# Softmax totals of a gated cross-attention block: the cross-partition sum moved from two 512-column matmuls to VectorE and two 16-column matmuls

## What is computed

```
x = x + tanh(g_xattn) * attention(layernorm(x), ctx, ctx, mask)

q, k, v = query @ Wq, key @ Wk, value @ Wv        # 32 query heads, 8 key heads, size 128
logits  = 30 * tanh(rope(q) . rope(k) * 0.0884 / 30)
logits  = where(mask, logits, -1e30)
weights = softmax(logits, axis=-1)                # needs the sum of exp over the keys
attn    = weights @ v ; return attn @ Wo
```

## Time and profile before

| | us |
|---|---|
| median of 3 runs | 819.16 |
| lowest and highest | 818.01, 819.62 |
| the profiled execution, device time | 819.05 |
| its span in the profile | 817.3 |

### The profile page before, as it was taken

The page is one execution under the profiler, slowest core; times in us unless marked ns, Lnnn a source line. Parts: engine busy times, 40 slices in busy tenths (PEclk is TensorE's granted clock), DMA queues, the critical chain, the costliest instruction groups (busy, mean ns, idle before and its releaser), DMA issues.

```text
span 817.3 us, 12587 instructions
## 1 busy us (share of the span) xinstructions
PE 785.6 (96%) x3937; PEld 654.8 (80%) x3937; DVE 586.6 (72%) x1224; ACT 355.4 (43%) x722; POOL 492.8 (60%) x392
## 2 busy tenths in 40 slices
PE   4889999999999999999999999999998689999998
PEld 3777888888888888888888888888887468888786
DVE  7797777777777777777777777776787677787531
ACT  3665444444334444444443443434444345555420
POOL 3689765566555666655665566656887466566400
PEclk9999999999999999999999999999999899999999
DMA  8320302010210201020102101120020034442011
GB/s 286 108 78 17 115 1 78 1 52 1 78 54 1 78 1 52 1 78 0 55 1 78 52 0 43 35 47 1 1 62 0 25 88 103 101 111 49 1 65 39
DMA packets 56989, 41.61 MB, mean 51 GB/s; under 512 B 22922, under 2 KB 44298, under 8 KB 56938
## 3 DMA queue, kind: packets, MB, share of 16 engines
q1 hardware_dynamic: 56938, 40.90, 17.3%
HBM read 38.77 MB, written 2.11 MB: 50 GB/s over the span
## 4 chain that ended last, share of the span: by engine, by line
PE 91%; DVE 5%; POOL 2%; issue 1%; ACT 1%; DMA 0%; DVEq 0%; POOLq 0%
PE ps_o L53 8%; PE ps_o L55 8%; PE ps_o L54 7%; PE bank_q L55 7%; PE bank_q L53 7%; PE bank_q L54 7%; PE ps_qT L1141 3%; PE bank_kv L53 3%; PE bank_kv L54 3%; PE bank_kv L55 3%; PE ps_s L54 3%; PE ps_s L53 3%; PE ps_s L55 3%; PE ps_pv L53 2%; PE ps_pv L54 2%; PE ps_pv L55 2%
## 5 line engine op out<-in xcount | busy, mean ns | idle before, releaser
L522 POOL TENSOR_TENSOR aT_lo<-attn,aT_hi 128x512 fp32r<-128x512 f32 x64 | 96.6, 1510 | 168.4 <-ACT aT_hi L691 168.4
L651 ACT CAST qT_hi<-ps_qT 128x512 fp32r<-128x512 f32 x64 | 37.5, 585 | 169.7 <-PE bank_kv L1142 90.0
L53 PE MATMUL bank_q<-wq_hi,xT_hi 128*128 128x512 f32 x256 | 107.7, 421 | 1.0 <-DVE wq_lo L819 1.0
L53 PE MATMUL ps_o<-wo_hi,aT_hi 128*128 128x512 f32 x256 | 100.6, 393 | 2.5 <-POOL aT_lo L522 1.8
L55 PE MATMUL bank_q<-wq_hi,xT_lo 128*128 128x512 f32 x256 | 102.3, 400 | 0.0
L54 PE MATMUL bank_q<-wq_lo,xT_hi 128*128 128x512 f32 x256 | 102.3, 400 | 0.0
L55 PE MATMUL ps_o<-wo_hi,aT_lo 128*128 128x512 f32 x256 | 99.9, 390 | 0.0
L54 PE MATMUL ps_o<-wo_lo,aT_hi 128*128 128x512 f32 x256 | 99.8, 390 | 0.0
L507 POOL TENSOR_TENSOR probs<-probs,keepT 128x512 f32<-128x512 f32 x64 | 83.1, 1299 | 13.0 <-ACT probs L667 13.0
L535 POOL TENSOR_TENSOR roped<-q_cos,q_sin 128x512 f32<-128x512 f32 x61 | 78.8, 1293 | 1.8 <-DVE q_sin L840 1.7
L911 DVE TENSOR_TENSOR qT_lo<-ps_qT,qT_hi 128x512 fp32r<-128x512 f32 x64 | 44.2, 691 | 43.4 <-ACT kT_hi L652 43.4
(11 more groups left out here) (233 smaller groups left out, 2209.5 us busy)
## 6 DMA issues: line engine op xcount, KB each, us to landing
wo_raw<-in_Wo SPq DMA_DIRECT2D x8, 1024.0 KB, 5.4
wq_raw<-in_Wq SPq DMA_DIRECT2D x7, 1024.0 KB, 5.7
packed<-in_gate_q SPq DMA_DIRECT2D x40, 64.0 KB, 2.3
packed<-in_up_q SPq DMA_DIRECT2D x40, 64.0 KB, 2.3
packed<-in_down_q SPq DMA_DIRECT2D x10, 256.0 KB, 3.4
acc<-in_x SPq DMA_DIRECT2D x8, 256.0 KB, 8.1
wkv_raw<-in_Wk SPq DMA_DIRECT2D x8, 256.0 KB, 5.9
wkv_raw<-in_Wv SPq DMA_DIRECT2D x8, 256.0 KB, 6.3
```

Of the source, the lines that this page charges most:

```text
L53: nc.tensor.matmul(out, w_hi, m_hi, start=first, stop=False)
L522: nc.gpsimd.tensor_tensor(aT_lo[:], attn[:], aT_hi[:].bitcast(F32), ALU.subtract).then_inc(a_split, 1)
L651: nc.scalar.copy(qT_hi[:], ps_qT[:])
```

## The change

The sum over the keys is taken in two steps. VectorE transposes the masked `probs` in blocks of 32x32 (into `r_tot`), which brings the 32 keys of a block of partitions onto the columns, and sums each group of 32 columns: a tile `partial` of 16 columns, in which row 32g + r holds what key group g gives to query r of each block of 32 queries. It is split into `partial_hi` and `partial_lo` on VectorE. A 128x128 matrix `fold` (one where row and column agree modulo 32, built on VectorE out of the identity at the start) sums the four key groups in two matmuls of 16 columns. The totals arrive in `ps_tot` already in the layout that the block transpose L960 made before, so that transpose goes and the reciprocal reads `ps_tot` directly. The new VectorE work stands behind `p_lo` and ahead of q's rotary products in the queue; TensorE waits for it (`p_summed`) ahead of the totals, and for `fold` ahead of its first slot, in place of `ones`. New semaphores are left out below.

```
@@ tiles
-        ones = sb("ones", [P, P], F32R)
+        fold = sb("fold", [P, P], F32R)
+        partial = sb("partial", [P, GC // 32], F32)
+        partial_hi = sb("partial_hi", [P, GC // 32], F32R)
+        partial_lo = sb("partial_lo", [P, GC // 32], F32R)
@@ GpSimd, start
-                nc.gpsimd.memset(ones[:].bitcast(F32), 1.0).then_inc(ones_done, 1)
@@ ScalarE, cap_and_exp
                     wait(act, p_split, j - 1)
+                    wait(act, p_turned, j - 1)
@@ VectorE, start
                 norm_moments(2)
+                dve.wait_ge(id_done, 1)
+                nc.vector.reduce_sum(r_tot[:, 0:32], ident[:].rearrange("p (i c) -> p c i", i=4), AX_X).then_inc(fold_done, 1)
+                dve.wait_ge(fold_done, 1)
+                nc.vector.tensor_copy(fold[:].rearrange("p (i c) -> p i c", i=4),
+                                      r_tot[:, 0:32].unsqueeze(1).to_broadcast([P, 4, 32])).then_inc(fold_done, 1)
                 dve.wait_ge(keep_T, 1)
@@ VectorE, slot, behind p_lo
+                    if runs(s - 2):
+                        wait(dve, masked, j - 1)
+                        wait(dve, norm_done, j - 2)
+                        nc.vector.transpose(r_tot[:], probs[:, (s - 2) % 2, :]).then_inc(p_turned, 1)
+                        wait(dve, p_turned, j - 1)
+                        wait(dve, tot_done, j - 2)
+                        nc.vector.reduce_sum(partial[:], r_tot[:].rearrange("p (c e) -> p c e", e=32), AX_X).then_inc(partial_rounded, 1)
+                        wait(dve, partial_rounded, 2 * j - 3)
+                        nc.vector.tensor_copy(partial_hi[:], partial[:]).then_inc(partial_rounded, 1)
+                        wait(dve, partial_rounded, 2 * j - 2)
+                        nc.vector.tensor_tensor(partial_lo[:], partial[:], partial_hi[:].bitcast(F32), ALU.subtract).then_inc(p_summed, 1)
                     if runs(s):
@@ VectorE, slot, behind tot_done
                         wait(dve, norm_done, j - 2)
-                        nc.vector.transpose(r_tot[:], ps_tot[:]).then_inc(tot_turned, 1)
-                        wait(dve, tot_turned, j - 1)
-                        nc.vector.reciprocal(r_small[:], r_tot[:].rearrange("p (c e) -> p c e", e=32)[:, :, 0]).then_inc(inverted, 1)
+                        nc.vector.reciprocal(r_small[:], ps_tot[:, 0:GC // 32]).then_inc(inverted, 1)
@@ TensorE, ahead of the slots
-                pe.wait_ge(ones_done, 1)
+                pe.wait_ge(fold_done, 2)
@@ TensorE, slot
                         wait(pe, norm_done, j - 2)
                         if s == 2:
                             pe.wait_ge(tab_done, 1)
-                        nc.tensor.matmul(ps_tot[:], ones[:], p_hi[:], start=True, stop=False)
-                        nc.tensor.matmul(ps_tot[:], ones[:], p_lo[:], start=False, stop=True).then_inc(tot_done, 1)
+                        wait(pe, p_summed, j - 1)
+                        nc.tensor.matmul(ps_tot[:, 0:GC // 32], fold[:], partial_hi[:], start=True, stop=False)
+                        nc.tensor.matmul(ps_tot[:, 0:GC // 32], fold[:], partial_lo[:], start=False, stop=True).then_inc(tot_done, 1)
```

More of the change, by code:

```diff
@@ L224, in flamingo_block @@
         ld_wq, ld_wkv, ld_wo = sem("ld_wq"), sem("ld_wkv"), sem("ld_wo")
-        id_zero, id_done, ones_done, half_done = sem("id_zero"), sem("id_done"), sem("ones_done"), sem("half_done")
+        id_zero, id_done, half_done = sem("id_zero"), sem("id_done"), sem("half_done")
         stats_done, moments_done, var_done = sem("stats_done"), sem("moments_done"), sem("var_done")
@@ L241, in flamingo_block @@
         tot_done, inverted, norm_done = sem("tot_done"), sem("inverted"), sem("norm_done")
-        tot_turned, r_spread = sem("tot_turned"), sem("r_spread")
+        p_turned, p_summed, r_spread, fold_done = sem("p_turned"), sem("p_summed"), sem("r_spread"), sem("fold_done")
+        partial_rounded = sem("partial_rounded")
         a_rounded, a_split, o_done, acc_done = sem("a_rounded"), sem("a_split"), sem("o_done"), sem("acc_done")
```

## The result

| | before | after |
|---|---|---|
| median of the runs, us | 818.79 | 872.82 |
| lowest and highest | 818.01, 819.62 | 869.01, 876.41 |
| span of the profiled execution | 817.3 | 871.8 |

The ratio is 1.065 (95% interval 1.063 to 1.068). The forecast was 849, 815 to 862: the sign was right, the size 24 us too small and outside the range.

The account below looks back on a forecast made before the run. TensorE, holding 91% of the chain that ended last, was taken as the bound. From 819.05 us, start 5.5, early slots 5, loop 20.2 and end -0.4 add 30.3, giving 849, range 815 to 862 (own range 843 to 857, chance 0.57).

Parts of the forecast that it names:

- The pair: TensorE's two totals matmuls: 0.22 us instead of 0.47 with weight loads at 0.11 each, gaining 0.24 per slot without waits.
- The turns in the loop: Loop: cast and subtraction queue behind GpSimd, making 24 wq slots 0.72 us late and 24 wo slots 0.12, 20.2 in all.
- Rival A: VectorE's chain: only the subtraction takes turns with GpSimd, the cast does not; 823.6 us, chance 0.20.
- B: VectorE's chain: nothing waits, 16-column operations slip in between GpSimd's reads; 811 us, chance 0.15.
- C: TensorE's totals: a short fp32r matmul exposes its load's whole 0.187 us; 860 us, chance 0.08.
- The start: TensorE's first slot waits for `fold`, ready at 17.40, so the first slot moves later: 5.5 us, between 4 and 8.3.
- The early slots: Slots ahead of the loop: chain meets GpSimd's splitting operations and delays the totals; 5 us, between 2 and 8.
- The last slots and the drain: End of the attention: TensorE waits for nothing, six slots gain 0.24, drain loses about 1 us; -0.4 in sum.

Follow-up runs that it names:

- e2: The changed kernel with the 16 partial sums in PSUM, in unused columns of the totals' bank, instead of SBUF; 827.59 us, ratio 1.010.
- e11: The kernel before with new totals in slots 7 to 55 only, partial sums in SBUF, loop written out, no wait at the start; 839.39 us, ratio 1.026.
- e6: The kernel before with the loop over the 48 middle slots written out; 818.54 us, ratio 1.000.
- e1: The changed kernel with TensorE's wait for `fold` moved from ahead of its first slot to the first use in the third slot; 865.95 us, ratio 1.058.
- e10: The changed kernel with partial sums in PSUM, the late wait for `fold` and the middle loop written out, new totals in all slots; 813.80 us, ratio 0.994.
- e3: The changed kernel with only the cast of the partial sums moved from VectorE to ScalarE; 849.69 us, ratio 1.039.
- e4: The kernel before with the four new VectorE steps added behind `p_lo`, their result unused and the old totals kept; 839.00 us, ratio 1.025.
- e7: The changed kernel with partial sums in PSUM and the late wait for `fold`, new totals in all slots, loop kept; 818.50 us, ratio 1.001.
- e8: The kernel before with new totals in slots 7 to 55 only, partial sums in PSUM, no wait at the start, loop kept; 811.84 us, ratio 0.992.
- e9: The kernel before with new totals in slots 7 to 55 only, partial sums in PSUM, no wait at the start, loop written out; 808.04 us, ratio 0.987.

## Why the prediction was wrong in size

**The pair, right.** Forecast 0.22 with 0.24 gained. Undisturbed slots are 9.12 in the mean, 0.22 less than 9.34. TensorE in time in e2:

```profile
304.71 0.17 PE L1211 MATMUL ps_tot<-partial_hi,fold 128*128 128x16 f32 x1
304.74 0.26 PE L1212 MATMUL ps_tot<-partial_lo,fold 128*128 128x16 f32 x1
304.85 0.48 PE L53 MATMUL ps_pv<-p_hi,v_hi 128*128 128x512 f32 x1
305.17 0.40 PE L54 MATMUL ps_pv<-p_lo,v_hi 128*128 128x512 f32 x1
```

0.14 lie before `ps_pv`, and its first matmul takes 0.32 until the next instead of 0.23: loads pass at 0.11 each. By the Trainium skill, "TensorE: Matmul & The Clock Gate", Back-to-back issue gap, whose floor of 25 ns is without the load, the pair would have been 0.05; the two matmuls do start 0.03 apart, but their weight loads and the next one start 0.11 apart (304.71, 304.82, 304.93).

**The turns in the loop, right.** Forecast 20.2 (slots of 10.06 and 9.46), measured 21.6 by the slots and by e11 against e6. Cast, `wkv_lo` and subtraction took their turns in the order written. Rival A (only the subtraction takes turns) and B (nothing waits) fall by the cast's 1.05, C by the pair's 0.23.

**The start, right.** `fold` was to be ready at 17.40 and was at 17.53; the product was to end at 22.7. TensorE and VectorE in time (it answers to the earlier trace rows):

```profile
17.58 0.79 PE L53 MATMUL bank_q<-wq_hi,xT_hi 128*128 128x512 f32 x1 [9.38 <-DVE fold L834]
```
```profile
17.30 0.23 DVE L834 CAST fold<-r_tot 128x128 fp32r<-128x128 f32 x1
...
22.63 0.69 DVE L847 TENSOR_TENSOR q_cos<-bank_q,q_tab 128x512 f32<-128x512 f32 x1 [4.91 <-PE bank_q L55]
```

**The early slots, wrong by 4.6.** The step that failed is "in the next four it is about 0.2, 0, 0.8 and 0.2", less 1 that GpSimd was to absorb. By slots, from the second to the eighth, the differences were 0.8, 2.7, 0.8, 1.7, 4.0, -0.2 and -0.2. The third was forecast at 2.9, the fourth at 2.0, so these two together came out 1.4 cheaper; the fifth and sixth, priced at 0.2 less what GpSimd was to absorb, cost 5.7. In the fifth TensorE waited 1.98 for `partial_lo`. The sixth shows both things missed. VectorE in time, then GpSimd:

```profile
83.60 1.19 DVE L949 CAST partial_hi<-partial 128x16 fp32r<-128x16 f32 x1
84.82 1.19 DVE L951 TENSOR_TENSOR partial_lo<-partial,partial_hi 128x16 fp32r<-128x16 f32 x1
```
```profile
83.49 1.27 POOL L439 TENSOR_TENSOR xT_lo<-xn,xT_hi 128x512 fp32r<-128x512 f32 x1
84.72 1.27 POOL L439 TENSOR_TENSOR cT_lo<-xn,cT_hi 128x512 fp32r<-128x512 f32 x1
```

TensorE in time:

```profile
86.16 0.25 PE L1211 MATMUL ps_tot<-partial_hi,fold 128*128 128x16 f32 x1 [2.71 <-DVE partial_lo L951]
...
86.81 0.63 PE L54 MATMUL ps_pv<-p_lo,v_hi 128*128 128x512 f32 x1
87.23 0.63 PE L55 MATMUL ps_pv<-p_hi,v_lo 128*128 128x512 f32 x1
```

Each of the two small operations stands behind a whole splitting operation, and TensorE waits 2.71. The rest goes with a slower clock. The sixth slot before and after, busy time by engine (window, its length, then PE, PEld, DVE, ACT, POOL with counts, granted clock, DMA share, GB/s), first of the kernel before:

```profile
65.27:75.78 10.51, 10.51 (x58) 8.70 (x58) 8.50 (x20) 6.59 (x14) 9.47 (x9) 1.00 0.00 1
```
```profile
76.94:91.47 14.53, 11.81 (x58) 9.76 (x57) 12.48 (x23) 6.59 (x14) 11.01 (x10) 0.88 0.00 1
```

The same number of matmuls holds TensorE for 11.81 instead of 10.51: 14.53 - 10.51 is 2.71 of wait and 1.30 of longer busy time, at a granted clock of 0.88 against 1.00, a mixture of the two levels: right behind the wait, from 86.81 to 89.80, the matmuls stand 0.42 to 0.43 apart, later 0.23. Over all early slots the clock fell from 0.99 to 0.90 and TensorE's busy time rose from 66.3 to 71.2 us. By slots the clock was 0.78 in the fourth, behind a wait of 2.72 for `partial_lo` at the end of the third, and 0.88 in the fifth and sixth, with waits of 1.98 and 2.71; before, all three were at 1.00. The wait of 9.4 at the start isn't the reason: e1 is without it and has 0.90 over the early slots as well, and e2 has one of 9.96 and shows 0.95. What can be put down to it is the second slot's 0.8, at 0.80 against 0.88 before and 0.88 in e1. I had priced the waits, and not that matmuls behind them can run slower. In e2, with shorter waits, the sixth slot is 10.47 at 1.00.

**The loop's jump, left out: 5.5.** The step that failed is the loop's sum, "24 x 0.72 and 24 x 0.12, 20.2 us": it takes every slot as regular and so puts the jump at nothing, without a reason. In the change VectorE has 2.84 and 2.54 us of `issue` at the jumps, and TensorE waits 2.00 and 2.07 us there instead of 0.65. In the kernel before VectorE's idle time at the same place is 0.93 and 0.90, released by ScalarE's `kT_hi`, where other slots have 0.58. So its trace shows no gap of 2.8 that something hid; why VectorE's gap is so much longer in the change isn't shown.

**The last slots and the drain, wrong by 12.7.** The step that failed is "TensorE waits for nothing: six slots at 0.24, less about 1 us for the drain". Behind the loop's stretch four slots gained (9.09 to 9.29), less than 0.8 in all. With that gain taken off, 4.3 are lost up to the last slot's transposes, 6.7 in the drain, and 1.2 in the feed-forward. VectorE in time in the drain:

```profile
668.59 0.70 DVE L944 STREAM_TRANSPOSE r_tot<-probs 128x512 f32<-128x512 f32 x1
669.33 0.69 DVE L947 TENSOR_REDUCE partial<-r_tot 128x16 f32<-128x512 f32 x1
670.04 0.31 DVE L949 CAST partial_hi<-partial 128x16 fp32r<-128x16 f32 x1
670.39 1.21 DVE L951 TENSOR_TENSOR partial_lo<-partial,partial_hi 128x16 fp32r<-128x16 f32 x1
```

TensorE's totals stand at 671.75 with 2.81 of idle time before them, and the next at 679.57 with 3.46. There VectorE's queue, not TensorE's, sets the time: the chain stands behind `attn`, `xn` and `xT_lo` and its full length is exposed, with the cast behind GpSimd's `acc` and the subtraction behind its mask. Here the clock fell too: from 616.59 to 637.98 before it was 1.00, over the same work after (663.13 to 691.24) 0.88. By e2 and e10 the chain's own length is worth 3.4 to 4.2 of the 12.3; turns with GpSimd, and the slower clock with them, are the rest, 8.9 as the difference of the change and e2. With the spread of this stretch, 9.6 to 14.8 in like kernels, that is a rough figure.

The sum: 0.2, 4.6, 5.5 of jumps with 1.4 of turns and -0.2 in one slot, and 12.7 are the 24.2 by which the span's difference (54.5) passed the forecast's 30.3.

The forecast's own range is mis-added as well. The ends given for the start (4 and 8.3) and for the early slots (2 and 8) lead to 844.5 and 855, and not to 843 and 857; the measured time lies outside either.

What stays open is what sets the cost of a jump. It was 0.5 in all before, 6.0 in the change, 2.8 in e1, 7.8 in e2, 7.9 in e3, 4.0 in e4, 5.2 in e7 and 3.1 in e8, kernels whose loops differ little. A part of the spread is the clock: it was 0.87 in the slots behind the wait in the change and e2, 0.86 in e3, and 1.00 in e1, e4, e7 and e8. Why it fell in some and not in the others, and why the `issue` stands on VectorE in the change, e1 and e2, on both engines in e4, on TensorE in e3 and e8, and on one at the first jump and the other at the second in e7, no run shows.

## What to carry to other kernels

A tiny VectorE operation with SBUF operands can cost a whole operation of GpSimd, and two that depend on each other can cost two: where a bank has columns free, keep the intermediates of such a chain in PSUM. A change that is judged in the steady slot needs its price in the others too: where the queue of the engine that gets the work is full (first and last slots, the drain) or another delay falls on it (a loop's jump), its steps are no longer covered. And wherever a new wait stops TensorE for microseconds, look at the granted clock of the stretch behind it, since the matmuls there can slow down as well; use the new way only in slots where its cover is shown, as e9 does.

## What the runs showed of the hardware

- Work of 16 columns on VectorE took 0.17 us undisturbed, in the cast and the subtraction alike, and behind GpSimd 1.05 and 0.65 in the loop's wq slots and up to 1.28 in the early ones; moving its input to PSUM was enough to end that.
- A sum over 128x512 took 0.69 with its result in SBUF and in PSUM.
- A loop's jump showed up to 3.1 us of `issue` on VectorE or up to 2.7 on TensorE, and cost 0.2 to 4.0 us; with the loop written out it was gone.
- The same wait of 2.0 us at a jump was followed by a granted clock of 0.87 over that slot in one kernel and of 1.00 in another (13.02 against 11.43 us).
- With waits of 2.72, 1.98 and 2.71 us for the totals TensorE's granted clock averaged 0.90 over the 81 us of the early slots, against 0.99 in the kernel before, and it was 0.88 in a drain with waits of 2.81 and 3.46, against 1.00.
